# A scatter that carries the edge attribute rows, and a gather of relation rows moved to the stage that sums them

## The reference, cut to what matters

```
edge_index = stack([src, dst])
x = layernorm(x + L0(x, edge_index, edge_weight))       # two rounds: segment_sum(x[src] * weight, dst)
x = layernorm(x + L1(x, edge_index))                    # segment_sum over src of x[dst] @ W_msg
x = layernorm(x + L2(x, edge_attr_128, edge_index))
x = layernorm(x + L3(edge_index, edge_type, x, rel_emb))  # two rounds

def L2(x, edge_attr, edge_index):
    agg = segment_sum(edge_attr, dst, 50000)            # this is the edge stage l2
    h = silu(LN(concat([x, agg]) @ W1 + b1))            # this is the node stage d2b
    return x + (h @ W2 + b2)

def L3_round(x):
    rel = rel_emb / max(norm(rel_emb), 1e-6)            # 1001 rows
    h_rel = rel[edge_type]                              # one relation row for each edge
    h = x[src] - 2 * dot(x[src], h_rel) * h_rel
    ... segment_sum(h, dst), divided by the degree, @ W, + x, LN
```

## Time and profile before

| what | value |
|---|---|
| median of 3 runs | 4827.94 us (4824.14 to 4830.65) |
| profiled execution, its own time | 4823.27 us |
| its span | 4821.5 us |
| PE, DVE, ACT, POOL busy | 78%, 74%, 45%, 66% of the span |
| front | 0 to 419 us |
| stages l2 and d2b | 2353 to 2637, and 2637 to 3430 us |
| DMA | 861.31 MB, mean 179 GB/s |

### The profile page before, as it was taken

One profiled execution on the slowest core, in us unless ns is written; L12 is line 12 of the kernel. 1 busy time (PEld: TensorE's weight loads), 2 busy tenths in 40 slices (PEclk: granted clock), 3 DMA queues, 4 the chain that ended last, 5 costly groups with the idle time before them and its releaser, 6 DMA issues.

```text
span 4821.5 us, 94015 instructions
## 1 busy us (share of the span) xinstructions
PE 3775.1 (78%) x18956; PEld 2297.9 (48%) x18956; DVE 3546.8 (74%) x13545; ACT 2185.7 (45%) x4510; POOL 3181.8 (66%) x3644
## 2 busy tenths in 40 slices
PE   4652789968899868899778889998578775787776
PEld 1221338833455523566433778888333442234443
DVE  8874646676487864576743788888887888887888
ACT  0000353314588844455335344444236564265666
POOL 4655757767599977333575566666576777775787
PEclk6876999989999989999899999999799998899999
DMA  1001468834688744688546455555356885477676
GB/s 24 10 8 36 131 207 275 279 104 149 213 272 259 233 133 153 222 270 272 168 129 209 131 166 172 165 169 164 107 164 219 251 249 172 144 222 238 222 236 198
DMA packets 481460, 861.31 MB, mean 179 GB/s; under 512 B 86745, under 2 KB 91584, under 8 KB 481048
## 3 DMA queue, kind: packets, MB, share of 16 engines
q1 hardware_dynamic: 335370, 596.71, 39.2%
q10 hardware_dynamic: 85310, 155.79, 8.8%
q0 software_dynamic: 60368, 104.48, 8.4%
HBM read 532.31 MB, written 324.36 MB: 178 GB/s over the span
## 4 chain that ended last, share of the span: by engine, by line
PE 30%; DVE 20%; issue 13%; POOL 12%; DVEq 7%; DMA 5%; SPq 3%; ACT 1%; POOLq 1%; ACTq 0%
PE ps L1425 10%; POOL got L635 7%; DVEq L65 6%; DVE hit L975 4%; DVE stat L1022 4%; PE ps L1548 3%; PE ps L1547 3%; PE ps L1453 2%; PE ps L1557 2%; DVE hid L1123 2%; POOL x2T L651 2%; POOL rstd L671 2%; DVE mv L1028 2%; PE ps L1485 2%; PE ps L1484 2%
## 5 line engine op out<-in xcount | busy, mean ns | idle before, releaser
L671 POOL TENSOR_TENSOR rstd<-vare,neg_half 128x4 f32<-128x4 f32 x686 | 698.8, 1019 | 627.5 <-DVE vare L1035 624.6
L1425 PE MATMUL ps<-hit,got 128*128 128x512 bf16 x1758 | 701.1, 399 | 476.0 <-DVE hit L975 310.9
L1199 ACT ACTIVATE evac<-ps 128x512 f32<-128x512 f32 x588 | 351.2, 597 | 1001.9 <-PE ps L1425 984.5
L1425 PE MATMUL ps<-hit,rest 128*128 128x512 bf16 x1758 | 702.6, 400 | 0.0
L1425 PE MATMUL ps<-hit,tail 128*128 128x512 bf16 x1758 | 700.8, 399 | 0.0
L1223 ACT ACTIVATE xout<-res,shift,rstd 128x128 f32<-128x128 f32 x1176 | 482.8, 485 | 431.5 <-POOL shift L674 411.9
L1425 PEld LDWEIGHTS ps<-hit,got 128*128 x1758 | 178.0, 101 | 855.2 <-issue 712.2
L1063 DVE TENSOR_TENSOR nT<-sums,ps 128x512 f32<-128x512 f32 x490 | 336.1, 686 | 325.0 <-PE ps L1463 269.6
L635 POOL DMA_INDIRECT got<-nodes_l,sorted_by_dst x392 | 395.5, 1009 | 164.5 <-issue 108.2
L975 DVE TENSOR_SCALAR hit<-node_of,node_at_dst 128x512 bf16<-128x512 f16 x1465 | 438.2, 367 | 19.3 <-POOLq L394 10.0
L1004 DVE TENSOR_TENSOR rest<-got 128x512 f32<-128x512 f32 x294 | 204.7, 696 | 240.2 <-DMA got<-in_edge_attr,sorted_by_dst 112.6
(11 more groups left out here) (264 smaller groups left out, 9163.2 us busy)
## 6 DMA issues: line engine op xcount, KB each, us to landing
nodes_l<-xout SPq DMA_DIRECT2D x196, 256.0 KB, 3.0
xin<-nodes_l SPq DMA_DIRECT2D x196, 256.0 KB, 2.7
sums_l<-evac ACTq DMA_DIRECT2D x196, 256.0 KB
sums<-sums_l SPq DMA_DIRECT2D x196, 256.0 KB
sums_l0a<-evac ACTq DMA_DIRECT2D x98, 256.0 KB
sums<-sums_l0a SPq DMA_DIRECT2D x98, 256.0 KB
sums_l0b<-evac ACTq DMA_DIRECT2D x98, 256.0 KB
sums<-sums_l0b SPq DMA_DIRECT2D x98, 256.0 KB
```

Of the source, the lines that this page charges most:

```text
L671: pool.tensor_tensor(rstd[:, n, at, :], vare[:, n, at, :], neg_half[:, :], ALU.pow)\
L1199: act.activation(evac[:, slot, :], ps[:, g % BANKS, :], ACT.Copy).then_inc(s["out"].sem, 1)
L1425: last = pe.matmul(into, part.rearrange("p a d -> p (a d)"), hit[:, i % HITS, :], start=False, stop=False, skip_group_check=True)
```

## The change

The records of the sort by `dst` become 136 words (544 bytes): the 8 words and the 128 words of the edge's attribute row. ACT loads the attribute rows in the front, a batch of four tiles at a time, into a ring of eight batches (`row`); each load again takes 127 partitions, with a second small one for the last partition in the first 27 batches. POOL waits for a batch, copies the 8 words of each record beside its row, waits for that copy, and scatters from `row`; the `pause` and the drain are gone. The reload of the 8 words reads them out of the 544-byte rows. The records by `src` stay as they are.

In `l2` SP loads the batches of attribute rows from the sorted records by plain DMAs; each load from the fifth on waits for POOL's word (`free`) that the ring slot is clear. POOL gathers the relation rows in this stage, and stores them, two batches behind. In `d2b` POOL keeps only the two chains, now in a loop. `rel_get` shares its memory with `rel`. The membership table of the two sorts shares one buffer; some buffers move. The diff also brings the class `Window` with a pair mode that no stage uses (`single` is the only instance, with `pair` false), so the extra loops run once.

```diff
-RECORD = {"dst": FIELDS, "src": FIELDS}
+RECORD = {"dst": FIELDS + D, "src": FIELDS}
+        def attr_parts(b):
+            v, full, k = t["edge_attr_128"], FULL_PARTS * TILES, b * K
+            held = row[:, b % ROW_RING, :, FIELDS:FIELDS + D].bitcast(F32)
+            parts = [(held[0:FULL_PARTS, :, :], v[0:full, :].rearrange("(p k) d -> p k d", k=TILES)[:, k:k + K, :])]
+            if k + K <= REST:
+                parts.append((held[FULL_PARTS:FULL_PARTS + 1, :, :], v[full + k:full + k + K, :].rearrange("(a k) d -> a k d", a=1)))
+            return parts
...
 # ACT, front
             act.dma_start(rel_in[:, :, :], t["L3_gnn_rel_emb"].rearrange("(p r) d -> p r d", r=11)).then_inc(s_rel_in, 16)
+            for b in range(BATCHES):
+                if b >= ROW_RING:
+                    act.wait_ge(s_scat[b % 4], 64 * (b // 4 - 1))
+                for part, ap in attr_parts(b):
+                    act.dma_start(part, ap).then_inc(s_row[b % ROW_RING], 16)
             act.wait_ge(s_cdve, 3)
             reload(act, "dst")
...
 # POOL, as_placed(b)
-                pool.memset(pause[:, :], 0.0)
-                pool.drain()
+                pool.wait_ge(s_row[b % ROW_RING], rows_in(b))
+                pool.tensor_copy(row[:, b % ROW_RING, :, 0:FIELDS], record[:, b * K:b * K + K, :]).then_inc(s_joined, 1)
+                held(s_joined, b + 1)
+                return lambda k: row[:, b % ROW_RING, k % K, :]
...
 # SP, edges(l2)
+                if WINDOWS[name][3] == "rows":
+                    attr = rec_d["dst"].rearrange("(p k) f -> p k f", p=P)
+                    for b in range(BATCHES):
+                        if b >= 4:
+                            sp.wait_ge(*s["free"](b - 3))
+                        at = b * K % RING
+                        sp.dma_start(single.got[0][:, at:at + K, :].bitcast(I32), attr[:, b * K:b * K + K, FIELDS:FIELDS + D])\
+                          .then_inc(s[f"line{b % 4}"].sem, 16)
...
 # POOL, edges(l2), for each batch b
                         held(s["step"].sem, free[j % 4] & 511)
+                        if kind == "rows":
+                            pool.sem_inc(s["free"].sem, 1)
+                    if kind == "rows":
+                        rel_rows(2 * b)
+                        rel_rows(2 * b + 1)
+                        if b >= 2:
+                            rel_store(b - 2)
+                        continue
...
+                if kind == "rows":
+                    rel_store(BATCHES - 2)
+                    rel_store(BATCHES - 1)
+                    for b in range(4):
+                        held(rel_put[b], 16 * len(range(b, BATCHES, 4)))
...
-            beside(8, d2b)
+            beside(8, lambda: pipeline(pool, GROUPS, 8, [(power("d2b", 1, "hst", "hrs"), 4), (power("d2b", 0, "var", "rstd"), 9)]))
```

More of the change, by code:

```diff
@@ L185, in __call__ @@
                 return held
-        front = Arena()
+        front = Arena(base)
         total_row = {n: front(f"total_row_{n}", [1, GROUPS]) for n in ("dst", "src")}
@@ L232, in program @@
         low_f = {n: front(f"low_{n}", [P, TILES]) for n in ("dst", "src")}
-        member = {n: front(f"member_{n}", [P, TILES, GROUPS], BF16) for n in ("dst", "src")}
+        member = front("member", [P, TILES, GROUPS], BF16)
+        row = front("row", [P, ROW_RING, K, FIELDS + D], I32)
         in_eight = front("in_eight", [P, 8, GROUPS])
@@ L242, in program, with __init__ @@
         junk = front("junk", [P, 28, GROUPS], BF16)
-        pause = front("pause", [P, 100])
         low_hit = front("low_hit", [P, 4, ROWS], BF16)
         parts = {n: front(f"parts_{n}", [GROUPS, 3, ROWS], BF16) for n in ("l0", "l1", "l3")}
[L246 to L258, removed]
+        class Window:
+            def __init__(self, name, at, hits, evacs, pair):
+                held = Arena(at)
+                self.hits, self.evacs, self.pair = hits, evacs, pair
+                self.hit = held(f"hit{name}", [P, hits, ROWS], BF16)
+                self.got = [held(f"got{name}{n}", [P, RING, D]) for n in range(1 + pair)]
+                self.rest = [held(f"rest{name}{n}", [P, RING, D]) for n in range(1 + pair)]
+                self.tail = [held(f"tail{name}{n}", [P, RING, 2 * D], BF16) for n in range(1 + pair)]
+                self.evac = [held(f"evac{name}{n}", [P, evacs, ROWS]) for n in range(1 + pair)]
+                self.got_hi = [buf[:, :, :].bitcast(BF16) for buf in self.got]
+                self.rest_hi = [buf[:, :, :].bitcast(BF16) for buf in self.rest]
+                self.end = held.at
+        single = Window("", base, HITS, EVAC, False)
+        late = Arena(single.end)
+        rel = late("rel", [P, 4, K, D])
+        prod = late("prod", [P, K, D])
+        dot4 = late("dot4", [P, 2, K])
+        node = Arena(base)
         xin = node("xin", [P, 8, K, D])
@@ L313, in program @@
         s_scat = [sem(f"s_scat{b}") for b in range(4)]
+        s_row = [sem(f"s_row{b}") for b in range(ROW_RING)]
+        s_joined = sem("s_joined")
         s_scattered = sem("s_scattered")
@@ L433, in edge_parts, with rows_in @@
                     (tile[FULL_PARTS:FULL_PARTS + 1, 0:REST], v[full:E].rearrange("(a k) -> a k", a=1))]
+        def attr_parts(b):
[5 more added lines that the diff above has]
+            return parts
+        def rows_in(b):
+            return 16 * sum(1 + (i * K + K <= REST) for i in range(b % ROW_RING, b + 1, ROW_RING))
         def reload(engine, name):
@@ L579, in _, with scatter @@
             pool.drain().then_inc(s_const, 1)
-            def scatter(name, between):
+            def scatter(name, rows):
                 n = SORTS.index(name)
@@ L609, in as_turned @@
                 held(*node_s["d0"]["tx"](2 * b + 1))
+                return lambda k: record[:, k, :]
             def base_of(n, b):
@@ L676, in power @@
                 return stage
[L678 to L705, removed]
             def beside(n, work):
@@ L986, in edges @@
                 for b in range(BATCHES):
-                    dve.wait_ge(*s[f"got{b % 4}"](64 * (b // 4 + 1)))
+                    arrived = s[f"line{b % 4}" if kind == "rows" else f"got{b % 4}"]
+                    dve.wait_ge(*arrived(ARRIVE[name] * (b // 4 + 1)))
                     if kind == "weight":
@@ L1003, in edges @@
                         dve.drain()
-                    dve.tensor_tensor(four(rest, b), four(got, b), upper(got_hi, b), ALU.subtract)
+                    for n in range(1 + w.pair):
+                        dve.tensor_tensor(four(w.rest[n], b), four(w.got[n], b), upper(w.got_hi[n], b), ALU.subtract)
                     dve.drain()
-                    dve.tensor_tensor(four(tail, b)[:, :, 0:D], four(rest, b), upper(rest_hi, b), ALU.subtract).then_inc(s["msg"].sem, 1)
+                    for n in range(1 + w.pair):
+                        last = dve.tensor_tensor(four(w.tail[n], b)[:, :, 0:D], four(w.rest[n], b), upper(w.rest_hi[n], b), ALU.subtract)
+                    last.then_inc(s["msg"].sem, 1)
                     hits(min(32 + 18 * (b + 1), b * K + K + NEED))
@@ L1436, in edges @@
                     for j in range(min(K, STEPS - K * q)):
-                        products(K * q + j, row[j], row[K + j])
+                        products(K * q + j, of[j], of[K + j])
                     if q + 1 < FOURS:
-                        row = numbers(step_tab, q + 1, 0, 2 * K)
+                        of = numbers(step_tab, q + 1, 0, 2 * K)
                         if q % 2:
```

103 lines of the change are left out of this document (66 added, 37 removed).

## The result

The changed kernel takes 5121.8 us (median of 4 runs, 5118.02 to 5125.12) against 4826.04 (4 runs): a ratio of 1.0612, 95% interval 1.0594 to 1.063. It is slower by 296 us. Its profiled execution took 5120.0 us, with a span of 5118.2.

The account below looks back on a forecast made before the run. POOL's scatter was taken to bound the front and POOL l2; after the change, loads on one DMA engine bound the front. Front +327, l2 +30, d2b -5 sum to +352: 5180 us, range 5010 to 5410.

Parts of the forecast that it names:

- One DMA engine for a 127-partition load: Front: all 49 attribute loads run on the same single DMA engine, so POOL waits for each batch; front +327 us.
- The first rival: Front: loads spread over many engines and POOL still sets the front; -14 us, 4814 us in all; chance 0.10.
- The batch: Front: 13.3 us of load plus 0.8 of scatter on one engine, 14.1 us (11.4 to 18.1); 49 make 691.
- the second rival: Front: a piece costs 40 ns whatever its size; front +694 us, about 5545 us in all; chance 0.06.
- The batch of 9.0 us: Front: at the skill page's 27 GiB/s per engine, 9.0 us a batch and a front some 120 us longer.
- Start, end and reload: Front: first load at 20.7 us, 9 after the last load, reload 20 (12 to 35), 4.7 to l0a.
- The copy for pause and drain: Front: POOL's own period falls from 6.8 to about 5.7 us, hidden by the loads, counted as nothing.
- l2: Stage l2, paced by POOL: 48 us of stores, less 12 of PE waits and 5 at the end, +30 (+10 to +45).
- The third rival: l2 gets shorter because its rows come 3 us after SP's issue: -20 instead of +30, 5130 us; inside the main case's chance.
- d2b: Stage d2b: gathers and stores leave POOL, outside the bounding ring; DVE's normalising may gain; -5 us (-12 to 0).
- The signs: Trace marks named beforehand: front near 750 us, POOL's waits 14 us apart, l2 305 to 325, d2b within 12 of 793.
- the two waits: Front: POOL waits for a `row` load before nearly every batch; DVE waits several hundred us for the sorted records.

Follow-up runs that it names:

- two-piece run: On the changed kernel, each attribute load of the front cut into two of 64 floats a row over the same 127 partitions: 5229 us (one run).
- the second experiment: On the changed kernel, relation gathers and stores moved back to d2b, plain loads kept in l2: 5088.8 us, ratio to the kernel before 1.0543.
- copy a batch ahead: Spread loads plus gathers in d2b, and POOL copies batch b+1's 8 words before scattering batch b: 4725.9 us (0.9788); 5182.5 on the slower chip.
- two gains together: Changed kernel with front loads cut into 112 and 15 partitions and relation gathers back in d2b: 4762.8 us (0.9865); 5059.5 on the slower chip.

## Why the prediction was right

The forecast was +352 us (5180), the result +296 (5122), inside the range of 5010 to 5410.

- **One DMA engine for a 127-partition load: right, and shown.** ACT's queue fills 1.09 engines; 112 + 15 partitions remove the wait, 113 + 14 bring it back, two loads over the same 127 do not help. That all 49 loads take the same engine follows too: loads of several batches are in flight, and on different engines they would have shown more than 1.09. This rests on experiments. The Trainium skill's rule ("DMA: Bandwidth & Descriptors", section "Why a DMA increments its semaphore by 16 and not by 1"), the largest divisor up to 16 of the partition count, agrees with all three: 16 engines for 112, one for 113 and for 127; the share of 0.75 of the 91-partition load lies under its 13 of 16. The first rival is gone; had I believed the 0.06 of the front alone, I would have forecast no change or a gain.
- **The batch: 14.1 us forecast, 13.3 measured.** The price of a piece was oversized: I scaled the 40 ns of the earlier trace rows by bytes to 26 and added the scatter's 0.8 us on top, but the measured 13.3 includes the scatter, and the packets start 24 ns apart. The 40 ns are the time in which a packet is in work, its overlap with its neighbour included. From the first load to the last copy it was 662 us instead of 691, 29 of the 56 us that I forecast too much. The two-piece run gives 3.4 ns a piece and the rest by bytes, so the second rival (40 ns whatever the size) was far off. The batch of 9.0 us that stands beside my sum was not reached either.
- **Start, end and reload: 20.7 + 9 + 20 + 4.7 forecast.** First load at 21.3, reload issued 7.6 us after the last copy (683.2), 16.7 for the reload, 4.5 to the stage. Front in all 746 and 712. The 20 for the reload was a choice between 7 and 63, without a row of its kind; that it came near is in part luck.
- **The copy for pause and drain: 5.7 us forecast as POOL's own period, 5.8 measured** once the loads were out of the way. It was hidden in the changed kernel, as said.
- **l2: +30 forecast, +13 measured.** The mechanism holds: POOL paced it, and without POOL's gathers it is 254 us. The term that was mis-sized is the store, which I took from d2b with its gap of 0.35 us; here all 49 stores have 2.3 us of idle time before them. 49 x 0.98 = 48 became 31 us of POOL time, and its waits for PE went down by 9 instead of 12. POOL's time grew by 24 us in all, and 11 of these did not lengthen the stage, where I had counted 5 for its end. The third rival (an l2 that gets shorter) needed just what the second experiment did.
- **d2b: -5 forecast, -8 measured.** DVE's normalising has a median of 405 ns and a maximum of 429, against 407 and 631 before; DVE is busy for 624 us instead of 631, and for 630 again with the gathers back. Two microseconds of the eight are not traced to an operation.
- **The signs.** The period, the two waits and d2b came as described. Two signs did not: the DMA share in the middle of the front is 0.14 and not a little above 0.06, because POOL's scatter of 544-byte rows adds 6.2% of sixteen engines, a share that I had left out; and l2 is 295 us with 5.9 us a batch, not 305 to 325 with 6.1.
- **What the change was worth without its flaw.** Its idea, plain loads in l2, gives 29 us there; its front costs 12 us in the reload and gains 1 us a batch by the lost pause. With the loads spread and the gathers left in d2b, where POOL has time, it is ahead of the kernel before (4762.8 against 4828.2), but that gain is the pause: the kernel before without its pause takes 4754.1. Only with the copy a batch ahead does carrying the rows in the scatter pay for itself (4725.9).

## What to carry to other kernels

Before a transfer is called hidden, count the DMA engines that it runs on: a mean DMA share of 0.06 is also what one engine at its limit shows, and the partition count of the tile decided here between 13.3 us and some 2 us for a batch's loads. Work that is moved to an engine costs what it adds to the stage that this engine paces: the same gathers cost 8 us in d2b and 42 us in l2. A delay that stands in every batch of a bounding chain is worth removing by itself; here a clear and a drain took 71 us in one pair of runs and 74 in the other.

## What the runs showed of the hardware that was not expected

DVE's membership operations (two inputs in SBUF, 5.1 us each) hold up POOL's indirect DMAs. In the kernel before:

```profile
187.01 20.37 DVE L755 TENSOR_TENSOR member_src<-iota_t,bin_f 128x4802 bf16<-128x4802 f32 x4
187.57 5.43 POOL L589 DMA_INDIRECT records_by_dst<-record,place_dst  x1 [0.30 <-issue]
193.31 4.77 POOL L589 DMA_INDIRECT records_by_dst<-record,place_dst  x1 [0.30 <-issue]
```

Beside them most of POOL's indirect DMAs take 4.8 us and up to 5.8 instead of 0.96, and POOL's small copy 4.3 instead of 0.22 (in the kernel with 112 + 15 partitions); in the unpaused kernels four operations of POOL are caught and some 15 to 17 us are lost. Each of these DMAs ends 0.8 to 0.9 us after one of DVE's four operations: the first of those ends at 187.01 + 5.1 = 192.1, the DMA at 193.0.

That DVE is the cause, and not the place in POOL's own sequence, shows where the slower chip moved the two apart. In the kernel with the two gains together DVE came to these operations 84 us later than on the other chip, and POOL's long operations moved with them:

```profile
272.82 20.37 DVE L802 TENSOR_TENSOR member<-iota_t,bin_f 128x4802 bf16<-128x4802 f32 x4
274.02 4.79 POOL L629 DMA_INDIRECT records_by_dst<-row,place_dst  x1 [0.30 <-issue]
288.95 4.31 POOL L643 COPY row<-record 128x32 int32<-128x32 int32 x1
```

With the copy ahead, DVE came to them at 404.07 us, behind the last scatter (334.75), and none of the 196 scatters took over 1.73 us:

```profile
L629 POOL DMA_INDIRECT records_by_dst<-row,place_dst x196: 957/962/1728, 58.4 to 334.8; - x196
```

The Trainium skill, "SBUF — State Buffer", section "SBUF: two separate sides", describes a pair of ports that DVE and GpSimd hold exclusively, and has DVE operations of this kind contend only with reads of GpSimd. The trace agrees for POOL's copy, which reads SBUF; an indirect DMA takes its indices from SBUF and could be such a read, but no run here shows which part of its work waits.

One place ran the kernel before and the kernel with the two gains together 6% slower (5115 against 4828 us, 5060 against 4763) and the kernel with the copy ahead 10% (5183 against 4726), with holds of up to 16 us on PE that no event of the core ends. It turned the order of the kernels round: the fastest of them elsewhere was 1.2% slower than the kernel before there. So a kernel is only read beside the kernel before on the same chip, and one chip may not be enough.
